# Stacking four heads' rows together in DRAM: seven transfers per stack, and score blocks one projection block later

## The reference, cut to what matters

```python
qkv = hidden_states @ w_attn + b_attn
q, k, v = jnp.split(qkv, 3, axis=-1)          # each reshaped to (B, S, 32, 16)
scores = jnp.einsum('bqhd,bkhd->bhqk', q, k) * SCALE
bias = slopes[:, None, None] * (pos[None, :] - pos[:, None])[None, :, :]
scores = jnp.where(causal, scores + bias, -jnp.inf)
attn = jax.nn.softmax(scores, axis=-1)
out = jnp.einsum('bhqk,bkhd->bqhd', attn, v).reshape(B, S, HIDDEN)
return out @ w_proj + b_proj
```

## Time and profile before

| | before |
|---|---|
| median of 3 runs | 940.39 us (939.13 to 942.77) |
| profiled execution: time / span | 939.05 / 937.2 us |
| PE busy | 855.5 us (91%) |
| DVE busy | 762.1 us (81%) |
| ACT busy | 439.2 us (47%) |
| POOL busy | 262.6 us (28%) |
| SP's transfers | 53.56 MB, 21.7% of 16 DMA engines |

### The profile page before, as it was taken

The page is one execution under the profiler, slowest core; times in us unless marked ns, Lnnn a source line. Parts: engine busy times, 40 slices in busy tenths (PEclk is TensorE's granted clock), DMA queues, the critical chain, the costliest instruction groups (busy, mean ns, idle before and its releaser), DMA issues.

```text
span 937.2 us, 12092 instructions
## 1 busy us (share of the span) xinstructions
PE 855.5 (91%) x4165; PEld 410.1 (44%) x4165; DVE 762.1 (81%) x1624; ACT 439.2 (47%) x828; POOL 262.6 (28%) x213
## 2 busy tenths in 40 slices
PE   3787978899978998799999999999999999999996
PEld 2334524454427453344444444444434444444442
DVE  6589999999996876598899989998245799776776
ACT  2667655656652031100666666667541656433100
POOL 1047899999994000031000000000001334000000
PEclk8689799999999999899999999999999999999999
DMA  9200060300006006820552255310015000000001
GB/s 347 94 1 0 1 269 1 134 1 1 0 1 201 0 29 151 197 69 1 87 78 47 34 77 78 53 29 1 2 39 202 1 0 0 1 0 1 12 34 46
DMA packets 27238, 54.34 MB, mean 58 GB/s; under 512 B 5876, under 2 KB 12660, under 8 KB 25896
## 3 DMA queue, kind: packets, MB, share of 16 engines
q1 hardware_dynamic: 27176, 53.56, 21.7%
HBM read 44.96 MB, written 8.39 MB: 57 GB/s over the span
## 4 chain that ended last, share of the span: by engine, by line
PE 62%; DVE 6%; DMA 1%; POOL 1%; SPq 1%; ACT 1%; issue 0%; POOLq 0%
PE ps L1135 16%; PE ps L997 7%; PE ps L1146 6%; PE ps L979 6%; PE ps L1019 5%; PE ps L963 4%; PE ps L966 3%; PE ps L1056 3%; PE ps L908 3%; PE ps L1036 3%; PE ps L982 2%; DVE ps L1403 1%; PE ps L747 1%; PE ps L902 1%; DMA stack<-in_alibi 1%; PE ps L911 1%
## 5 line engine op out<-in xcount | busy, mean ns | idle before, releaser
L700 ACT ACTIVATE prob<-ps 128x512 f32<-128x512 f32 x288 | 160.1, 599 | 124.4 <-PE ps L982 96.2
L468 POOL TENSOR_TENSOR hC<-hs,C_sb 128x512 f32<-128x512 f32 x128 | 162.1, 1283 | 59.3 <-DVE hs L1288 51.3
L889 PE MATMUL ps<-hC,identf 128*128 128x512 f32 x256 | 136.1, 634 | 24.1 <-POOL hC L468 22.9
L979 PE MATMUL ps<-stack 123*128 123x512 bf16 (+3 forms) x384 | 113.8, 327 | 0.2
L636 ACT ACTIVATE ps<-dtT,nA 128x512 f32<-128x512 f32 x128 | 88.2, 689 | 47.5 <-DVE hs L1288 47.5
L424 POOL TENSOR_TENSOR rstd<-veps,mhalf 128x4 f32<-128x4 f32 x8 | 8.1, 1012 | 358.4 <-DVE veps L1173 358.4
L1410 DVE TENSOR_REDUCE mrow<-ps 128x1 f32<-128x512 f32 x128 | 82.0, 683 | 11.4 <-PE ps L966 11.2
L889 PEld LDWEIGHTS ps<-hC,identf 128*128 128x128 f32 x256 | 44.0, 194 | 90.0 <-POOL hC L468 77.3
L997 PE MATMUL ps<-prob,V 128*32 128x512 f32 (+3 forms) x768 | 81.6, 498 | 0.7 <-ACT prob L700 0.7
L1135 PE MATMUL ps<-hT,wg 128*128 128x512 f32 (+1 forms) x176 | 79.1, 592 | 0.0
L1135 PE MATMUL ps<-hT,wu 128*128 128x512 f32 (+1 forms) x176 | 79.1, 592 | 0.0
(11 more groups left out here) (194 smaller groups left out, 1334.1 us busy)
## 6 DMA issues: line engine op xcount, KB each, us to landing
stack<-parts_dram SPq DMA_DIRECT2D x96, 128.0 KB
wmod<-in_wmod SPq DMA_DIRECT2D x4, 1536.0 KB, 11.3
parts_dram<-qkp SPq DMA_DIRECT2D x16, 384.0 KB, 2.7
wmod<-in_wmod SPq DMA_DIRECT2D x4, 1024.0 KB, 9.8
wattn<-in_wattn SPq DMA_DIRECT2D x1, 3072.0 KB, 10.0
wg<-in_wg SPq DMA_DIRECT2D x1, 2752.0 KB, 12.3
wu<-in_wu SPq DMA_DIRECT2D x1, 2752.0 KB, 10.5
wd<-in_wd SPq DMA_DIRECT2D x1, 2560.0 KB, 11.4
```

The costliest lines, as they stand in the source:

```text
L468: pool.tensor_tensor(hC[:, c, :], hs[:, c, :], C_sb[:, m % 2, :], ALU.mult).then_inc(S["hc_done"], 1)
L700: A_(prob[:, u % 4, j, :], ps[:, 3 + F % 3, :], ACT.Exp).then_inc(S["exp_done"], 1)
L889: mm(ps[:, c, :], identf[:], hC[:, c, :], start=False, stop=(s == NS - 1), skip_group_check=True).then_inc(S["sum_done"], 1)
L979: ins = mm(ps[:, bank, col:col + w], qk[0:ATT_ALL, 1, j, tile(kb)], qk[0:ATT_ALL, 0, j, q0:q0 + w], start=True, stop=not diag)
```

## The change

1. On the host the first 1024 columns of w_attn and the elements of b_attn are permuted: within each group of four heads the column order becomes dimension first, head second. In parts_dram the four heads of one dimension are then neighbours, and one partition of a stack is one run of 8 KB.
2. load_stack makes seven transfers in place of 13. The strips are taken as three sets, (first strip, count) = (0, 3), (3, 2), (5, 1). For each set one transfer brings Q parts 0 to count-1, and one brings a single K part (3 - count) to `count` strips by a broadcast. The order of the products in the strips changes with it; the six pairs are the same.
3. The ALiBi rows are stored as [8 groups][24][4 heads x 1024], one run of 8 KB for each row.
4. load_stack(0) is issued behind write 4 instead of write 5, load_stack(1) behind write 6 instead of write 7.
5. S_QK is 9: the score blocks start after block 9 (the tenth), and 11 instead of 12 are done by the end of block 15.

```diff
-S_QK = 8
+S_QK = 9
...
             def load_stack(g):
-                for o, order in ((0, PARTS_Q), (1, PARTS_K)):
-                    for b, part in enumerate(order):
-                        at_ = o * D + g * GH * HD
-                        load(stack[g % 3][16 * b:16 * b + 16, o, :, :],
-                             parts_dram[part, at_:at_ + GH * HD, :].rearrange("(h d) t -> d h t", d=HD), stk[g % 3])
-                load(stack[g % 3][ATT_K:ATT_S, 1, :, :].bitcast(U16),
-                     a["alibi"][g * GH:(g + 1) * GH, :, :].rearrange("h r t -> r h t"), stk[g % 3])
+                for first, count in ((0, 3), (3, 2), (5, 1)):
+                    at_ = g * GH * HD
+                    q = parts_dram[0:count, at_:at_ + GH * HD, :].rearrange("q (d h) t -> q d (h t)", h=GH)
+                    load(stack[g % 3][16 * first:16 * (first + count), 0, :, :], q, stk[g % 3])
+                    at_, part = D + g * GH * HD, 3 - count
+                    k = parts_dram[part:part + 1, at_:at_ + GH * HD, :].rearrange("q (d h) t -> q d (h t)", h=GH)                         .to_broadcast([count, HD, GH * T])
+                    load(stack[g % 3][16 * first:16 * (first + count), 1, :, :], k, stk[g % 3])
+                load(stack[g % 3][ATT_K:ATT_S, 1, :, :].bitcast(U16), a["alibi"][g], stk[g % 3])
...
-                if i == 5:
+                if i == 4:
                     for r in range(3):
                         sp.wait_ge(qk_wr[r], 16 * (2 if r < 2 else 1))
                     load_stack(0)
-                if i == 7:
+                if i == 6:
                     load_stack(1)
...
-                    pe.wait_ge(stk[g % 3], 16 * 13 * (g // 3 + 1))
+                    pe.wait_ge(stk[g % 3], 16 * 7 * (g // 3 + 1))
...
+    order = np.arange(2 * D).reshape(2 * NG, GH, HD).transpose(0, 2, 1).reshape(-1)
+    order = np.concatenate([order, np.arange(2 * D, 3 * D)])
+    b_attn = g["L1_attn_b_attn"][order]
...
-        wattn=c(g["L1_attn_w_attn"]), b_qk=cols(b_attn[0:2 * D]), b_v=c(b_attn[2 * D:]),
+        wattn=c(g["L1_attn_w_attn"][:, order]), b_qk=cols(b_attn[0:2 * D]), b_v=c(b_attn[2 * D:]),
```

More of the change, by code:

```diff
@@ L42 @@
 ATT_ALL = ATT_S + ATT_R
-PARTS_Q = (0, 0, 1, 1, 0, 2)
-PARTS_K = (0, 1, 0, 1, 2, 0)
 F32 = mybir.dt.float32
@@ L1555, in constants @@
     qconst = np.zeros((ATT_A, T), np.float32)
-    alibi = np.zeros((NH, ATT_A, T), np.uint16)
+    alibi = np.zeros((NG, GH, ATT_A, T), np.uint16)
     for b in range(NT):
@@ L1559, in constants @@
         for n, part in enumerate(three(sl[:, None] * (j - (b * P + 64)).astype(np.float32)[None, :])):
-            alibi[:, 3 * b + n, :] = part
+            alibi[:, :, 3 * b + n, :] = part.reshape(NG, GH, T)
     return {
@@ L1564, in constants @@
         "negm": bf16_bits(np.where(p[:, None] > p[None, :], -1e38, 0.0)),
-        "qconst": bf16_bits(qconst), "kones": bf16_bits(np.ones((ATT_R, T))), "alibi": alibi,
+        "qconst": bf16_bits(qconst), "kones": bf16_bits(np.ones((ATT_R, T))), "alibi": np.ascontiguousarray(alibi.transpose(0, 2, 1, 3)),
         "eidx": np.tile(np.arange(E, dtype=np.float32)[None, :, None], (P, 1, NR)),
@@ L1580 @@
     xpw[:, 32:64] = xp[RANK:].T
-    b_attn = g["L1_attn_b_attn"]
+    order = np.arange(2 * D).reshape(2 * NG, GH, HD).transpose(0, 2, 1).reshape(-1)
+    order = np.concatenate([order, np.arange(2 * D, 3 * D)])
+    b_attn = g["L1_attn_b_attn"][order]
     arrays = dict(
```

## The result

| | before | after |
|---|---|---|
| median | 940.9 us (939.13 to 942.77, 4 runs) | 1029.96 us (1027.82 to 1033.19, 4 runs) |
| profiled execution: span | 937.2 us | 1030.3 us |
| PE busy | 855.5 us (91%) | 877.8 us (85%) |
| DVE busy | 762.1 us | 764.6 us |
| SP's transfers | 53.56 MB, 21.7% of 16 engines | 53.55 MB, 15.5% |

The ratio is 1.0955, with a 95% interval of 1.0934 to 1.0975. The forecast was 1022 (930 to 1080), slower.

A forecast was written before the change was run, and what follows sets the result against it. PE, busy 855.5 of 937.2 us, was taken as the bound. Projection 24.7 + 1.4, stack 2 9.6 + 1.4, stacks 3 to 7 38.0 + 7 gave +82 on 939.05: median 1022, range 930 to 1080.

The forecast's parts named there:

- The number of engines: Stack loads: wide transfers leading with 3 or 2 use only 3 or 2 engines, always the lowest-numbered; 54 small packets.
- The time of a load: Stack load: engine 0 carries 68 rows at 22 GB/s, 25.3 us of data, 26.9 us from issue to landing.
- Projection: Late stack 0, then write 7 behind stack 1, delay PE's block 13: +24.7 us, plus 1.4 for the clock.
- Stack 2: Its load of 26.9 us exceeds the room of 17.3: +9.6 us, plus 1.4 for the clock.
- Stacks 3 to 7: Each load of 26.9 us exceeds the room of 19.3: 7.6 us five times, +38.0, plus about 7 for the clock.
- the slow clock: Behind a long PE wait the clock runs at its lower level: 1.4 us more for each wait.
- Sum: Whole kernel: all terms together add +82 us, taking the profiled 939.05 to 1021 and the median to 1022.
- Rival 1: Stack loads: engines 0 and 2 share a way into SBUF and halve each other; +124, 1064 us; chance 0.25 including beyond.
- a quarter of the crowding: Argument against shared-way slowing in stack loads: two engines on one way crowd a quarter as much as before's rows.
- Rival 2: Stack loads use all 16 engines and get faster, about 8 us of data; the 8.3 us wait goes: 931; chance 0.17.
- Rival 3: Stack loads spread evenly, data near 13 us; write 7 behind stack 1 takes back the early gain: 938 to 941; chance 0.05.
- The early score blocks: S_QK = 9 moves one score block of 0.2 us of PE into the V projection and hides nothing.

The follow-up runs named there:

- e3_k_strips: The changed kernel with K read strip by strip (six transfers of 16 rows), Q as changed, 10 transfers: 974.54 us, ratio 1.0358.
- e2_apart: The changed kernel with strip sets (2, 3), (0, 2), (5, 1), so simultaneously written strips are no longer 32 partitions apart: 1018.57 us, ratio 1.0825.
- e6_even: The changed kernel with another DRAM layout of the parts, so its seven transfers per stack lead with 48, 32 or 16 rows: 941.61 us, ratio 1.0005.
- e1: The changed kernel with each stack read strip by strip, 12 transfers of 16 rows plus ALiBi: 945.14 us, ratio 1.0051.
- e4: The kernel before with only the earlier loads (behind writes 4 and 6) and S_QK = 9: 942.14 us, ratio 1.0012.
- e5_late: The changed kernel with loads back behind writes 5 and 7 and S_QK = 8: 1029.81 us, ratio 1.0947.
- e8_before_s10: The kernel before with only S_QK changed, to 10: 940.42 us, ratio 1.0000.
- e11_stack1_late: The kernel before with S_QK = 10 and stack 1 issued behind write 13 instead of 7: 934.96 us, ratio 0.9941.
- e12_even_best: The even DRAM layout of e6_even with stack 0 behind write 4, stack 1 behind write 13, S_QK = 9: 935.42 us, ratio 0.9936.
- e10_even_late_s10: The even DRAM layout of e6_even with loads behind writes 5 and 7 and S_QK = 10: 936.74 us, ratio 0.9962.

## Why the prediction was right, point by point

**The number of engines.** Right, and it carries everything: 54 small packets were forecast for a stack and 54 are there. The rows of before had only transfers whose two sides lead alike; that a source leading with 3 binds a destination of 48 rows was the step beyond them, and it held, for 2 as well. The Trainium skill, "DMA: Bandwidth & Descriptors", section "Why a DMA increments its semaphore by 16 and not by 1", states the mixed case; the counts of 54, 129, 108 and 204 in these four kernels agree with it. The forecast also needed the few engines to be the same ones in all transfers. For stack 3 they were: laid end to end, its packets show one engine at work from 1.5 to 27.6 us behind the issue, on 68 rows, the 68 of the forecast.

**The time of a load.** Forecast 25.3 us of data and 26.9 from issue to landing; measured about 26 and 27.7 to 29.3 (28.1 for stack 3). The size was right within some 6%, the reason wasn't: I had all of engine 0's rows at 22 GB/s, halfway between two bounds, and no row spoke for the middle, so that part is luck. An engine goes at about 25 GB/s while few work and at about 8.4 while all work on 16-row strips, and some 2 us hang on where the strips lie. e3_k_strips, where the others work longer, found the error.

**Projection.** Forecast +26.1. The V projection starts at 434.79; before, it was here:

```profile
408.58 1.02 PE L1036 MATMUL ps<-wattn,hT 128*128 128x512 f32 x2
```

That is 26.2 later, of which 1.3 were there already at the first projection matmul (339.75 against 338.47): +24.9. The chain was as told: stack 0, then write 7 behind stack 1, then a maximum. One part of it I had not told: split 8 also waited 20.7 us, for write 5 behind stack 0; it lies beside PE's own wait of 15.9. Split 10 waited as forecast, for write 7:

```profile
417.19 0.43 DVE L1453 CAST qkp<-qkf 128x512 bf16<-128x512 f32 x1 [17.75 <-DMA parts_dram<-qkp]
```

The wait of PE for stack 0 was forecast from 375 to 391 and ended at 391.95; the next began behind block 12 and ended at 420.61, forecast 421.9.

**Stack 2.** Forecast +11.0. The issue of stack 2 moved from 448.95 to 476.12, that of stack 3 from 477.70 to 518.36: 27.2 and 40.7, so +13.5. **Stacks 3 to 7.** Forecast +9.0 a group; the issues of stacks 4 and 5 (508.49 to 559.85; 539.28 to 601.21) give +10.7 and +10.6, and the remaining three, to the end of the span, +31.1. Together 52.4 against 45. In both the mis-sized terms are two: the wait, 8.2 to 9.8 us instead of 7.6 (stack 3's load 1.2 us longer than forecast), and the slow clock behind it. Six waits are 53.6 us and the six groups lost 65.9, so 2.1 us each lie beside the wait and not 1.4. The slow clock accounts for them: 4.54 us of PE's work at 0.50 (546 to 551 us) is 2.3 us more than at 1.00. The price of 1.4 came from the block of 5.08 us in the earlier trace rows; even the same kind of block took 6.30 us in the changed kernel (the row at 392.78), 2.65 more than its 3.65, and in the groups the first five us ran at the lower level.

**Sum.** 24.9 + 1.3 (there already before the projection begins) + 13.5 + 52.4 + about 1 (between the V projection's start and stack 2) = 93.1 of span, forecast 82. The medians differ by 89.1: the changed kernel's profiled execution was 2.1 us above its median, that of before 1.9 us below.

**The rivals.** Rival 1 (1064): its effect exists but is a quarter of the size (e2_apart). Its arguments were thin: the third of the bandwidth in the earlier trace rows says that 16 partitions take less than 128, not what a pair 32 apart does, and "a quarter of the crowding" follows from no row. Rival 2 (931): didn't happen here; its premise, 16 engines for seven transfers, was built in e6_even and gave 941.6. Such a load takes 11.5 us and not 8, and PE waited 2.07 us for it and 4.4 for DVE in the place of the 8.3. Rival 3 (no gain by an even spread) is thereby the one that describes e1, e4 and e6. Its figure was 938 to 941; e6 is 0.6 and e4 1.1 us above it, e1 4 us.

**The early score blocks.** "S_QK = 9 hides nothing" was not tested alone: e5_late moves it back together with the loads, and the two together are worth nothing (1029.8 against 1030.0).

What stays open: why all 16 engines together move only 8.4 to 8.7 GB/s each into 16-row strips, and why the wider strips of e6_even are little better (169 GB/s at share 1.01 from 480.5 to 490 us, 10.5 for an engine).

## What to carry to other kernels

Before fewer, wider transfers are counted as a saving, look at the leading dimension of both sides: here a leading dimension of 3, a broadcast one too, put the whole transfer on 3 engines, and several such transfers met on the same ones. Then compare the time of the load on its busiest engine with the room between its issue and its first use in the steady loop, where a shortfall is paid in every turn. And on a shared queue ask what stands behind the load: here a write that a compute engine waits for took back each gain of an earlier load, and moving the load that nobody needed yet out of its way gave 5.5 us (e8_before_s10 to e11_stack1_late) and 6.2 us (e6_even to e12_even_best). The one gain without that move was 4.1 us (e10_even_late_s10).

## What the runs showed of the hardware that I had not expected

- Runs of 8 KB were no faster than runs of 2 KB on 16-row strips: 8.4 GB/s an engine in e1_strips, 8.7 in the kernel before.
- Three engines with wide rows beside idle ones kept 25 GB/s each, three times their share in a crowd of 16. It is the crowd on the strips and not the kind of transfer: the last nine rows of a load in e3_k_strips, 16-row transfers' and ALiBi's, took 309 to 338 ns each, most rows of e1_strips about 1 us. The seven uneven transfers occupy the engines less in all (15.5% against 21.7%) and finish later.
- The issuing queue is held as well: six issues took 15.36 us when their engines had a stack's rows queued, 3.8 to 4.5 otherwise.
